# A GRU stage fed tile by tile: gate inputs spread by four transfers in place of sixteen, one half of a pruned feed-forward moved to VectorE, a longer run of warming matmuls

## The reference, cut to what matters

```
# feed-forward, 1024 hidden values for each token
hidden = sigmoid(x @ w_gate) * (x @ w_gate) * (x @ w_up)
hidden = hidden * (one of the two largest |values| in its group of 4)
x = x + hidden @ w_down
# GRU, one state of 256 for each of 4 batches, 256 steps in order
gi = x[t] @ W_ih + b_ih ;  gh = h @ W_hh + b_hh
r = sigmoid(gi_r + gh_r) ; z = sigmoid(gi_z + gh_z) ; n = tanh(gi_n + r * gh_n)
h = (1 - z) * n + z * h
```

## Time and profile before

| | us |
|---|---|
| three runs | 1002.78, 1007.39 (median), 1009.81 |
| the profiled execution | 1011.21 |
| its span in the trace | 1008.9 |
| the GRU loop in it | about 494 (from 329.5 to 823.4) |

### The profile page before, as it was taken

How to read it: one execution, slowest core, us unless ns; L and a number is a source line. 1 busy time by engine, 2 the same in 40 slices (tenths; PEclk the granted TensorE clock), 3 DMA queues, 4 the chain that set the end, 5 groups by cost and what they waited for, 6 DMA issues and landing times.

```text
span 1008.9 us, 39463 instructions
## 1 busy us (share of the span) xinstructions
PE 774.1 (77%) x16555; PEld 512.8 (51%) x16648; DVE 612.4 (61%) x2104; ACT 476.6 (47%) x1905; POOL 414.0 (41%) x493
## 2 busy tenths in 40 slices
PE   3789977868997786967769597695666568999876
PEld 3444544445654564644546455464544445666554
DVE  5655555786647675676766667675675653343457
ACT  2523433376541564756656565564554533444231
POOL 0386670274136394592937739286002002211000
PEclk9999999899999897999999989998997999999989
DMA  8100000400000000000000000000013000000001
GB/s 252 32 1 2 2 1 1 156 1 1 2 22 11 4 5 12 5 15 4 8 11 4 13 4 13 6 5 14 4 17 115 4 3 1 2 1 2 1 1 42
DMA packets 33344, 20.14 MB, mean 20 GB/s; under 512 B 23953, under 2 KB 30097, under 8 KB 33169
## 3 DMA queue, kind: packets, MB, share of 16 engines
q1 hardware_dynamic: 27984, 17.04, 6.0%
q10 hardware_dynamic: 5184, 0.59, 0.4%
HBM read 14.47 MB, written 1.05 MB: 15 GB/s over the span
## 4 chain that ended last, share of the span: by engine, by line
PE 53%; DVE 24%; ACT 8%; issue 6%; SPq 2%; DMA 1%; POOL 1%; ACTq 0%; DVEq 0%; POOLq 0%
PE banks L1344 16%; PE banks L1289 5%; DVE work L1644 4%; DVE h_ring L1658 3%; PE banks L1314 3%; DVE gate_r L1640 3%; ACT nzh L1477 3%; DVE pre_n L1649 3%; PE banks L410 2%; PE banks L1688 2%; SPq L1269 2%; PE banks L385 2%; PE banks L318 2%; PE banks L1770 2%; PE banks L1744 1%
## 5 line engine op out<-in xcount | busy, mean ns | idle before, releaser
L1344 PE MATMUL banks<-w_qkv,h_ring 128*4 128x64 f32 x12288 | 233.2, 226 | 138.9 <-DVE h_ring L1658 125.4
L1344 PEld LDWEIGHTS banks<-w_qkv,h_ring 128*4 128x4 f32 x12288 | 182.9, 90 | 215.0 <-DVE h_ring L1658 197.3
L1468 ACT ACTIVATE banks<-gate_r 128x8 f32<-128x8 f32 x256 | 46.2, 181 | 186.7 <-DVE gate_r L1640 185.9
L1640 DVE STREAM_TRANSPOSE gate_r<-banks 128x64 f32<-128x64 f32 x256 | 64.0, 250 | 83.3 <-PE banks L1344 79.5
L1644 DVE STREAM_TRANSPOSE work<-banks 128x64 f32<-128x64 f32 x256 | 76.6, 299 | 6.8 <-PE banks L1344 6.5
L1658 DVE TENSOR_TENSOR_SCAN h_ring<-banks,nzh 128x24 f32<-128x24 f32 x256 | 52.9, 207 | 33.2 <-ACT nzh L1477 1.8
L1509 POOL TENSOR_TENSOR work<-work 128x512 f32<-128x512 f32 x14 | 17.8, 1271 | 127.4 <-ACT work L1405 127.4
L318 PE MATMUL banks<-zero 128*128 128x512 bf16 x192 | 61.9, 417 | 4.6 <-DVE work L2216 2.6
L1649 DVE TENSOR_TENSOR_SCAN pre_n<-banks,work 128x16 f32<-128x16 f32 x256 | 48.8, 191 | 27.3 <-DVE work L1644 1.4
L1473 ACT ACTIVATE gate_z<-banks 128x64 f32<-128x64 f32 x256 | 57.1, 223 | 12.6 <-PE banks L1344 12.2
L1651 DVE STREAM_TRANSPOSE banks<-gate_z 128x64 f32<-128x64 f32 x256 | 60.7, 237 | 2.9 <-ACT gate_z L1473 0.8
(11 more groups left out here) (446 smaller groups left out, 1651.5 us busy)
## 6 DMA issues: line engine op xcount, KB each, us to landing
big<-in_x SPq DMA_DIRECT2D x1, 1024.0 KB, 5.8
w_gate<-in_L_ffn_w_gate SPq DMA_DIRECT2D x1, 1024.0 KB, 4.9
shared<-in_L_ffn_w_down SPq DMA_DIRECT2D x1, 1024.0 KB, 7.5
w_gate<-in_L_ffn_W SPq DMA_DIRECT2D x1, 1024.0 KB, 5.5
shared<-in_L_ffn_W SPq DMA_DIRECT2D x1, 1024.0 KB, 10.4
out_x<-big SPq DMA_DIRECT2D x4, 256.0 KB, 2.4
w_qkv<-in_L_cond_W_qkv SPq DMA_DIRECT2D x1, 768.0 KB, 7.2
w_qkv<-in_L_attn_W_qkv SPq DMA_DIRECT2D x1, 768.0 KB, 9.0
```

What stands on the lines that cost most here:

```text
L1344: mm = nc.tensor.matmul(bank[32 * j:32 * j + B, 0:64], h_col(t, c), w_hh[:, c, g, :].rearrange("p (m n) -> p m n", m=KC)[:, :, 32 * j:32 * ...
L1640: nc.vector.transpose(gate_r[:, :], bank_r[:, 0:64]).then_inc(g_tr, 1)
```

## The change

- `rows_out` writes `g_tok` ordered by unit group j, then gate, so that the 128 values of one group stand together.
- `spread` moves one group j for all four batches at once: four transfers for a tile, each of 128 pieces of 512 B, from 128 partitions to 4. For tile 0 SyncE and ScalarE issue two each; for later tiles SyncE three, ScalarE one in step 24.
- Tile 1's first half is multiplied by VectorE straight from PSUM and compared, both before `grown(0, m)`; the rest of its pruning (`counted`, `kept_of`) stays where the whole of it was. ScalarE's two copies and GpSimd's two products of that half go.
- 36 warming matmuls ahead of the first step in place of 24.

```
-        RING, TILE, TILES, G2_DMAS = 64, 32, S // 32, 16
+        RING, TILE, TILES, G2_DMAS = 64, 32, S // 32, 4
...
-        def spread(op, tile, b, j):
-            return op.dma_start(g_row[tile % 2][32 * j + b:32 * j + b + 1, :, :, :].rearrange("p u g (m n) -> p u (g m) n", m=KC),
-                                g_tok[tile % 2][32 * b:32 * b + 32, :].rearrange("u (g n) -> u g n", g=4)[:, :, 32 * j:32 * j + 32]).then_inc(g_g2, 16)
+        def spread(op, tile, j):
+            return op.dma_start(g_row[tile % 2][32 * j:32 * j + B, :, :, :].rearrange("p u g n -> p u (g n)"),
+                                g_tok[tile % 2][:, P * j:P * (j + 1)]).then_inc(g_g2, 16)
...
-            keep_warm(24, bank_b)
+            keep_warm(36, bank_b)
...
-                if tile == 0:
+                if tile == 0 or (tile, n) == (1, 0):
                     a.then_inc(e_gc, 1)
...
             gate_sigmoid(1, 0)
-            gate_copy(1, 0)
             by_hidden_out(0, 0)
-            up_copy(1, 0)
             by_hidden_out(0, 1)
...
             for j in (2, 3):
-                for b in range(B):
-                    spread(nc.scalar, 0, b, j)
+                spread(nc.scalar, 0, j)
...
-                elif u in (24, 25, 26, 27) and tile + 1 < TILES:
+                elif u == 24 and tile + 1 < TILES:
                     act.wait_ge(g_gd, 4 * tile + 8)
-                    spread(nc.scalar, tile + 1, u - 24, 3)
+                    spread(nc.scalar, tile + 1, 3)
...
-            for n in range(2):
-                multiplied(pool, nc.gpsimd, chain, 1, n)
+            multiplied(pool, nc.gpsimd, chain, 1, 1)
             pruned_pool(pool, chain, 1, 1)
...
-                return nc.vector.tensor_tensor(g_tok[tile % 2][:, P * n:P * (n + 1)], bank_a[:, P * n:P * (n + 1)],
-                                               bias_rz[:, P * n:P * (n + 1)], ALU.add).then_inc(g_gd, 1)
+                cols = lambda a: a[:, P * n:P * (n + 1)].rearrange("p (j x) -> p j x", j=4)
+                return nc.vector.tensor_tensor(g_tok[tile % 2].rearrange("p (j g x) -> p j g x", j=4, g=4)[:, :, n, :], cols(bank_a),
+                                               cols(bias_rz), ALU.add).then_inc(g_gd, 1)
...
+            multiplied_at_once(v, chain, 1, 0)
+            compared(v, chain, 1, 0)
             for m in range(KC):
                 grown(0, m)
             for n in range(4):
                 rows_out(0, n)
...
-            pruned(v, chain, 1, 0)
+            counted(chain, 0)
+            kept_of(0)
...
             for tile in range(TILES):
                 sp.wait_ge(g_gd, 4 * tile + 4)
                 for j in range(2 if tile == 0 else 3):
-                    for b in range(B):
-                        spread(nc.sync, tile, b, j)
+                    spread(nc.sync, tile, j)
```

More of the change, by code:

```diff
@@ L1409, in up_copy @@
                 act.wait_ge(e_tr, 2 * tile - 1 + n)
-                nc.scalar.copy(kept[:, 512 * n:512 * (n + 1)], (bank_b, bank_a)[n][:, :]).then_inc(e_uc, 1)
+                nc.scalar.copy(kept[:, 512 * n:512 * (n + 1)], (bank_b, bank_a)[n][:, :]).then_inc(e_uc, 2 if tile == 1 else 1)
             def by_hidden_out(tile, n):
@@ L1497, in build, with multiplied_at_once @@
         quad = lambda a: a.rearrange("p (g e) -> p g e", e=4)
-        def multiplied_at_once(v, chain, n):
+        def multiplied_at_once(v, chain, tile, n):
             h, s = (a[:, 512 * n:512 * (n + 1)] for a in (hid, sgm))
-            v.wait_ge(e_gc, n + 1)
+            v.wait_ge(e_gc, 2 * tile + n + 1)
             chain.done(nc.vector.tensor_tensor(h, (bank_d, bank_c)[n][:, :], s, ALU.mult))
-            v.wait_ge(e_up, n + 1)
+            v.wait_ge(e_up, 2 * tile + n + 1)
             nc.vector.tensor_tensor(h, (bank_b, bank_a)[n][:, :], h, ALU.mult).then_inc(e_free, 1)
@@ L1511, in multiplied, with pruned, compared @@
             op.tensor_tensor(h, h, k, ALU.mult).then_inc(e_hid, 1)
-        def pruned(eng, chain, tile, n):
-            op = nc.vector
[L1515 to L1520, removed]
+        def pruned(v, chain, tile, n):
+            compared(v, chain, tile, n)
+            counted(chain, n)
+            kept_of(n)
+        def compared(v, chain, tile, n):
+            op = nc.vector
+            h, ab = (a[:, 512 * n:512 * (n + 1)] for a in (hid, sgm))
+            one, two, three = (a[:, P * n:P * (n + 1), :] for a in (c1p, c2p, c3p))
+            v.wait_ge(e_free, 2 * tile + n + 1)
             chain.done(op.tensor_scalar(ab.bitcast(I32), h.bitcast(I32), 0x7FFFFFFF, None, ALU.bitwise_and))
-            a4, h4 = quad(ab), quad(h)
+            a4 = quad(ab)
             op.tensor_tensor(one[:, :, 1:4], a4[:, :, 0:3], a4[:, :, 1:4], ALU.is_ge)
@@ L1525, in pruned, with counted @@
             chain.done(op.tensor_tensor(three, a4[:, :, 0:1], a4[:, :, 3:4], ALU.is_ge))
+        def counted(chain, n):
+            op = nc.vector
+            one, two, three, w = (a[:, P * n:P * (n + 1), :] for a in (c1p, c2p, c3p, win))
             chain.done(op.tensor_tensor(w, one[:, :, 1:5], one[:, :, 0:4], ALU.subtract))
@@ L1530, in pruned, with kept_of @@
             chain.done(op.tensor_tensor(w[:, :, 3:4], w[:, :, 3:4], three, ALU.subtract))
+        def kept_of(n):
+            h4, k4 = (quad(a[:, 512 * n:512 * (n + 1)]) for a in (hid, kept))
+            w = win[:, P * n:P * (n + 1), :]
             for e in range(4):
-                a = op.scalar_tensor_tensor(quad(k)[:, :, e:e + 1], w[:, :, e:e + 1], float(2 - e), h4[:, :, e:e + 1], ALU.is_ge, ALU.mult)
+                a = nc.vector.scalar_tensor_tensor(k4[:, :, e:e + 1], w[:, :, e:e + 1], float(2 - e), h4[:, :, e:e + 1], ALU.is_ge, ALU.mult)
             a.then_inc(e_kept[n], 1)
@@ L1540, in pruned_pool @@
             one, two, three, w = (a[:, P * n:P * (n + 1), :] for a in (c1p, c2p, c3p, win))
-            pool.wait_ge(e_hid, 2 * tile + n - 1)
+            pool.wait_ge(e_hid, 2 * tile + n - 2)
             chain.done(op.tensor_scalar(ab, h, 0.0, 2.0, ALU.is_ge, ALU.mult))
@@ L1619, in phase3_dve @@
             for n in range(2):
-                multiplied_at_once(v, chain, n)
+                multiplied_at_once(v, chain, 0, n)
                 pruned(v, chain, 0, n)
+            multiplied_at_once(v, chain, 1, 0)
+            compared(v, chain, 1, 0)
             for m in range(KC):
```

## The result

Twenty runs each: 997.14 us in the median (994.71 to 1002.37) where the kernel before has 1007.7 (997.73 to 1019.66). The medians lie 10.6 us apart. All ratios here leave out executions over 1.5% above the fastest of their kernel and group. This one, by the means, is 0.9912, 95% interval 0.989 to 0.9934: faster by 0.9%. The profiled execution took 996.6 us (span 994.8), 14.6 less than the one before. The forecast was 995.5.

The account below looks back on a forecast made before the run. The GRU loop was taken as a chain through three engines, losing time around tile boundaries. Gains of 4.8 (start), 3.4 and 7.3 sum to 15.5 us; 1011.2 less that is 995.7, stated as 995.5, range 987.5 to 1003.

Parts of the forecast that it names:

- VectorE's chain: Ahead of the loop: without GpSimd's products VectorE prunes faster and TensorE's 1.40 us idle goes; gain 1.4 us, bounds 0.4 and 1.4.
- The first tile's transfers: Ahead of the loop: tile 0's four transfers, carried by four engines at 28 ns a piece, land at 326.4, bounds 324.3 and 329.2.
- Warming: Ahead of the loop: 36 matmuls end at 326.1, TensorE idles 0.6 us, first steps run at 2.4 GHz; start in sum 4.8 us.
- Waits of the seeds and instruction stalls: At tile boundaries: ScalarE's waits for transfers go, 3.4 us; TensorE's missing-instruction stalls mostly go, 7.3 of 9.2 us.
- The last boundary: At the last tile boundary, where weight loads follow the transfers: the 5.1 us lost stays as it was, bounds 0 and 8.
- the rival of the held-up burst: At every tile boundary: larger pieces on four engines hold up TensorE's instructions; 9.6 us slower, 1020.8 us; chance 0.04.

Follow-up runs that it names:

- run 2: The kernel before with tile 1's first half on VectorE alone (sixteen transfers, 24 warming matmuls): 1009.0 us, ratio 1.002.
- run 1: The kernel before with the four transfers of 512 B pieces alone (24 warming matmuls, tile 1's first half on GpSimd): 999.0 us, ratio 0.990.
- run 11: The kernel before with only the piece size changed, sixteen transfers of 512 B pieces: 992.9 us, ratio 0.9866.
- run 5: The changed kernel with sixteen transfers of 512 B pieces, each from 32 partitions to 1, in place of four: 990.5 us, ratio 0.9843.
- run 3: The kernel before with 36 warming matmuls as the only change: 1010.6 us, ratio 1.003.
- run 4: The changed kernel with SyncE's 2.75 MB of weight loads held until the last tile's transfers have landed: 992.8 us, ratio 0.9851.
- run 6: The changed kernel with four transfers for a tile but 128 B pieces, in the old order in g_tok: 1012.7 us, ratio 1.0061.
- run 12: The kernel before with pieces of 256 B, sixteen transfers of 64 pieces, nothing else changed: 991.9 us, ratio 0.985.
- run 10: The changed kernel with sixteen transfers of 512 B pieces and each of three weight loads let go separately, in steps 4, 12 and 20: 988.5 us, ratio 0.9811.
- run 9: The changed kernel with sixteen transfers of 512 B pieces and weight loads held until the last tile's transfers have landed: 988.8 us, ratio 0.9821.

## Why the prediction was right, and where it was not

- *VectorE's chain.* Forecast 1.4 us; measured 2.5 from the hidden layer's first matmul to the gate inputs (22.3 us before, 19.7 in the changed kernel and in run 2). The idle 1.40 went as said, and the pruning of the second half took 4.8 us (304.63 to 309.44). The rest is TensorE's clock, which had fallen in L1314 in the profiled execution; against the traces where it had not (runs 1 and 11) this part is worth 1.6, so the term was well sized and the clock was left out. VectorE's added work fitted, with 3.1 us.
- *The first tile's transfers.* Four engines was right (132 packets), and so the rule of the Trainium skill, "DMA: Bandwidth & Descriptors", section "Why a DMA increments its semaphore by 16 and not by 1", that gave it. The price was not: 28 ns for a piece, between those of 128 B and 1 KB; measured 50 and 71 on four engines. It is 25 on sixteen (run 5), so the interpolation held for the size and missed that four engines work slower on each piece. 9.5 us to the release, not 8.4. That the first matmul came at 326.6 with 326.7 forecast is luck: this error and the clock's share above cancel.
- *Warming.* The matmuls ended at 324.6, and TensorE idled 2.0 us, not 0.6; the first steps were at full clock all the same. That the 36 did this is not borne out: alone they gave nothing (run 3), and run 4 lost the clock with them after 1.92 us.
- *Waits of the seeds and instruction stalls.* Forecast 3.4 and 7.3 of 9.2 us; all of it went, 12.7 in sum. The reason given had two parts. Less time with transfers under way is wrong: the changed kernel's traffic lasts as long as before, some 10 us (share 0.27 to 0.40 from 373 to 382), and run 6's lasts 12 us without such stalls. A quarter of the engines is not refuted: run 6 has no stall with 128 B pieces. But it isn't needed, for with sixteen engines the stalls go as well once the pieces are larger (runs 5, 11, 12). And fewer issues would not have ended the waits of the seeds: with 128 B pieces run 6 waits 12.5 us. The larger piece ended both. The forecast counted it only as a price for an engine, so that these two terms came out is in part luck.
- *The last boundary.* Forecast 5.1 left as it was, bounds 0 and 8; it is 8.4, just outside. This term was wrong. That the loads start earlier was seen, that they now meet the four-engine transfers was not counted; run 4 shows that this costs most of it. It is like the rival of the held-up burst, at one boundary in place of seven, but only where the loads join the transfers.
- *The sum.* Forecast 15.5, measured 14.6 between the two profiled executions and 10.6 between the medians. Between the two traces (14.1 us of span) it is 2.9 for the first matmul, 0.6 for its step and 1.2 for the seven intervals (forecast 4.8), 12.7 at six boundaries (10.7), less 3.3 at the last (0). The execution on which the sum was made had more stalls than the median run (1011.2 against 1007.7), and some of what was taken away was probably not there in most runs; no trace of a median run shows it.

What stays open is why pieces of 128 B hold up instructions that aren't in the same queue. The engines were not full (share 0.1 to 0.4), and at the stall at 390.19 they had moved no data for 3 us. What can be seen is the block of instructions ahead of it. It took 2.9 us (9.1% of 2 us times 16), the next one 0.9. The instruction queue of the kernel before from 386 to 388 and from 392 to 394 us:

```profile
q8 instruction: 1, 0.02, 9.1%
...
q8 instruction: 1, 0.02, 2.9%
```

Open too is why a piece costs twice as much when four engines carry it, and whether it is the four transfers or the four engines that spare run 6 the stalls. No run separates these.

## What to carry to other kernels

Look at the smallest piece of a transfer before its count: going from 128 B to 256 or 512 B took nearly all of the 17.7 us at the boundaries, while joining sixteen transfers into four put them on four engines and lost part of it again. TensorE's "issue" rows in the steps with transfers and just behind them are the sign, and the slow clock behind a stall can double the price (1.9 us of stalls in the stretch that lost 4.5). Large loads that nobody waits for belong away from transfers that four engines carry. Spread apart they stalled nothing (run 10), but in one burst behind the transfers they didn't either in run 9, and the times don't tell the two apart.

## What was not expected of the hardware

- Transfers inside SBUF with 128 B pieces release their waiter 4.9 to 6.3 us behind the last issue, with 256 or 512 B 2.6 us, at the same 0.6 us for an issue.
- Sixteen transfers of 128 B pieces went with stalls of TensorE for instructions in 18 of 28 stretches of four traces, four transfers of them (run 6) in none of seven.
- 512 B pieces on four engines kept all sixteen busy with loads at 75 to 140 GB/s; freed of them the loads ran at 370. TensorE stood 6.22 us meanwhile, and no block of instructions started for 12 us.
- With an idle time of 1.92 to 2.00 us ahead of the loop, the clock held in the changed kernel and fell one step later in run 4; with 1.39 to 1.42 us ahead of L1302 it fell in four traces and held in two. Whether a pause costs the clock can't be read from its length alone.
